# FFN output of six chunks: VectorE 32x32 block turns and SP transfers in place of TensorE transposes

## The chip, the cores and the metric

One core of a Trainium2 chip runs the whole program. The metric is the device time of one execution in microseconds; smaller is better. The kernel before was run three times: 540.84, 541.06 and 541.09 us.

## The reference

The input `x` is 2048 tokens by 128 features, fp32. Three residual steps follow each other, each on the layer-normed `x`:

```python
x = x + 0.5 * ffn(layernorm(x))      # FFN pass 1
x = x + attention(layernorm(x))      # one head, 2048 x 2048 logits
x = x + 0.5 * ffn(layernorm(x))      # FFN pass 2, same weights

# ffn: 64 experts of width 64, top 8 by biased affinity, plus one shared expert
h = silu(einsum('td,edf->etf', xf, W_up))
y = einsum('etf,efd->etd', h, W_down)
out = silu(xf @ Ws_up) @ Ws_down + einsum('etd,te->td', y, cw)
```

`cw` holds the normalised sigmoid gates of a token's eight experts and zero elsewhere. The kernel computes all experts for all tokens and multiplies by `cw`.

## The kernel before

An FFN pass works on four chunks of 512 tokens; chunks are numbered n = 0 to 3 in the first pass and 4 to 7 in the second, and c = n mod 4. In a chunk the tokens lie along the free dimension, the features or hidden rows on the 128 partitions. A chunk is 32 units of two experts each (u = 1 to 32), and a shared-expert unit only where c = 0. Every matrix product is three matmuls of 128x512 (high by low, low by high, high by high parts in the fp32r type).

One unit goes through all engines:

- TensorE: `up(u)`, three matmuls into one of four PSUM buffers, `hid[u mod 4]`; and five units later `down(u)`, three matmuls that accumulate the chunk's y in the PSUM bank `yacc[n mod 2]`. From u = 7 on `up` is issued in pairs, at odd u.
- ScalarE: silu of the hidden buffer (L451), later the high part of the gated product (L462).
- VectorE: `gate_unit`, silu times the gates in `wide` (L718), and the low part (L295) of every third unit (u = 6, 9, 12, 18 and so on). It runs its list strictly in order: the low part of unit u stands right behind the gating of unit u + 1.
- GpSimd: the low part of the other units (L295, and u = 15), out of the buffer `gated`.
- SP: two transfers per unit (L353), each spreading one expert's gates from DRAM over 64 partitions into one of six slots of `wide`. The transfers of unit u wait until unit u - 6 is gated. SP also issues the loads of x and of the weights, the store of the gates (`store_gates`, at u = 30) and the stores of the result. Nothing else is on it, and it also works its list in order.

`up(u + 4)` reuses the buffer of unit u. It waits (`wait_hid_free`) until unit u is gated where GpSimd makes its low part, and until VectorE has made its low part where VectorE does. So `up(16)` waits for the low part of unit 12, which VectorE makes behind the gating of unit 13; `up(22)` waits for the low part of unit 18, made behind the gating of unit 19.

Beside the units, hand-placed by the value of u, run the prologue of the next chunk (layer norm, affinities, top 8, gates: `pro_...`, `joint_...`; on VectorE mostly at u = 13 to 20, absent where c = 3) and the epilogue of the last one. The epilogue of y in chunks n = 1, 2, 3, 5, 6, 7 (it works on y of n - 1) is: ScalarE copies y from PSUM to `yT`, times 0.5, at u = 6 (`epi_y`, L502); TensorE transposes it in four 128x128 matmuls into the bank `mq` at u = 8 (`epi_yT`, through `turn`, L1279); VectorE adds `mq` to x at u = 9 (`epi_x`, L930). In the first pass only (n = 1 to 3), `epi_stats` at u = 10 takes the layer-norm statistics of the new x, four 128x128 pieces (L726, L733), and the keys of the attention follow from u = 20 on. The last chunk of a pass has its own epilogue in halves (`last_...`), in which `yT` is used as before.

The attention between the passes, some 130 us, needs nothing from SP.

Of the kernel before, what the change touches and what calls it, by code (L numbers as in the profile page):

```python
# [31 lines left out]
NB = 6  # L32
EARLY = 6
STORE = 30
GT = 2
# [13 lines left out]
def macaron_kernel(nc, x_d, wup_d, wdn_d, wsup_d, wsdn_d, cent_d, bias_d, wq_d, wk_d, wv_d, gates_d, out_d):  # L49
# [21 lines left out]
    with ExitStack() as ctx:  # L71
# [58 lines left out]
        gated = sb("gated", [P, NG, CH], F32, ffn)  # L130
        yT = sb("yT", [P, CH], F32, ffn)
        xn2 = sb("xn2", [P, TPC, D], F32, ffn)
        gpart = [sb("gpart_hi", [P, NGP, CH], F32R, ffn), sb("gpart_lo", [P, NGP, CH], F32R, ffn)]
# [23 lines left out]
        s_x0b = sem("x_in0_second_half")  # L157
        s_small, s_value, s_qk, s_bias = sem("small_in"), sem("value_in"), sem("qk_in"), sem("bias_in")
        s_eps, s_zero = sem("eps_made"), sem("cw_zeroed")
        j_out, j_aff, j_silu, j_hi, j_lo = (sem("shared_" + n) for n in ("and_aff", "aff_copied", "silu", "hi", "lo"))  # L160
# [152 lines left out]
        def _(sp):  # L313
# [18 lines left out]
            def store_gates(n):  # L332
                sp.wait_ge(s_gates, n + 1)
                sp.dma_start(gates_d[n], gates[:, :]).then_inc(s_gout, 16)

            for n in range(2 * NCH):
                if n % NCH == 0:
                    store_gates(n)
                sp.wait_ge(s_gout, 16 * (n + 1))
                for u in range(1, UNITS):  # L340
                    if early_unit(u, n):
                        continue
                    w = nth_gated(u, n)
                    if n == 0 and u % 2 == 1 and FIRST + (u - NB) // 2 < 2 * WP:
                        load_piece(FIRST + (u - NB) // 2)
                    if n == 0 and u in (24, 28):
                        load_x(u // 4 - 4)
                    if u == STORE and n % NCH != NCH - 1:
                        store_gates(n + 1)
                    if w > NB:  # L350
                        sp.wait_ge(s_gated, w - NB)
                    for e in range(2):
                        sp.dma_start(wide[e * F:(e + 1) * F, slot_of(u, n), :],  # L353
                                     gates_d[n, 2 * u - 2 + e, :].partition_broadcast(F)
                                     ).then_inc(s_wide[slot_of(u, n)], 16)
# [8 lines left out]
        def _(pool):  # L364
# [46 lines left out]
            for f in range(2):  # L411
                for c in range(NCH):
# [6 lines left out]
                    for u in range(min(c, 1), UNITS):  # L419
                        if on_pool(place(u, n)):  # L420
                            low_part(nc.gpsimd, place(u, n)).then_inc(s_glop, 1)
                        if n == 0 and u % 2 == 0 and PRE + u // 2 < 2 * WP:
                            piece_lo(PRE + u // 2)
                        if c + 1 < NCH:
                            if u == 3:
                                rstd(0, n + 1, p_st, p_rs)
                            if u == 18:
                                weights(n + 1)
                            if u == 21:
                                normed_weights(n + 1)  # L430
                        if f == 0 and c and u == 12:
# [7 lines left out]
        def _(act):  # L439
# [57 lines left out]

            def epi_y(n):
                act.wait_ge(s_down, place(PAIRS, n) + 1)
                if n:  # L500
                    act.wait_ge(e_yT, n)
                nc.scalar.mul(yT[:, :], yacc[n % 2][:, :], 0.5).then_inc(e_y, 1)  # L502

            def last_y(n):

                act.wait_ge(s_down, place(UNITS - LAG - 1, n) + 1)
                act.wait_ge(e_yT, n)
                nc.scalar.mul(yT[:, :], yacc[1][:, :], 0.5).then_inc(h_ya, 1)
# [57 lines left out]
            for f in range(2):  # L566
                for c in range(NCH):
# [21 lines left out]
                    for u in range(7 if n == NCH else min(c, 1), UNITS):  # L589
# [19 lines left out]
                        if c:  # L609
                            if u == LAG + 1:  # L610
                                epi_y(n - 1)
                            if f == 0 and u == 27:
                                epi_hi(c - 1)
                            if n == 1 and u == 31:
                                epi_proj_hi(0)
# [79 lines left out]
        def _(dve):  # L695
# [80 lines left out]
            def last_x(h, n, done):  # L776

                dve.wait_ge((h_yT, e_yT)[h], (n // NCH, n)[h] + 1)
                half = x[:, NT - TPC + h * GT:NT - TPC + (h + 1) * GT, :]
# [141 lines left out]
            def pro_sum(n):  # L921
# [4 lines left out]
                nc.vector.reciprocal(inverse_sum(n), wsum[:, 0, :]).then_inc(p_inv, 1)  # L926

            def epi_x(n, c):
                dve.wait_ge(e_yT, n + 1)
                nc.vector.tensor_tensor(x[:, c * TPC:(c + 1) * TPC, :], x[:, c * TPC:(c + 1) * TPC, :],  # L930
                                        mq[:, :].rearrange("p (t d) -> p t d", d=D), ALU.add).then_inc(e_x, 1)

# [39 lines left out]
            for f in range(2):  # L972
                for c in range(NCH):
# [25 lines left out]
                    for u in range(5 if n == NCH else min(c, 1), UNITS):  # L999
# [35 lines left out]
                        if c:  # L1035
                            if u == 9:
                                epi_x(n - 1, c - 1)
                            if f == 0:
                                if u == 10:
                                    epi_stats(c - 1)  # L1040
                                if u == 20:
# [3 lines left out]
                                if u == 21:  # L1045
                                    normed(1, c - 1, c - 1, xn2, e_rs, e_xn, (2, 3))
                                if u == 27:
# [123 lines left out]
        def _(pe):  # L1171
# [78 lines left out]
            def joint_product(n):  # L1250

                pe.wait_ge(p_lo, n + 1)
                if n % NCH > 1:
                    pe.wait_ge(e_x, n - 1)
                else:
# [46 lines left out]
            def pro_cw(n):  # L1302
# [3 lines left out]
                else:  # L1306
                    for i in range(TPC):
                        ins = nc.tensor.transpose(mp[0:E, i * P:(i + 1) * P], cw2[:, i, 0:E], ident[:, :])
                    ins.then_inc(p_cwT, 1)

            def epi_yT(n):
                pe.wait_ge(e_y, n + 1)
                pe.wait_ge(j_lo, joint(n + 1))
                if 0 < n < NCH:
                    pe.wait_ge(e_prlo, 1)
                    pe.wait_ge(e_lo, n)
                elif n == 0:
                    pe.wait_ge(w_Alo, 1)
                else:
                    pe.wait_ge(e_x, n)  # L1320
                turn(yT, mq, e_yT)

# [75 lines left out]
            for f in range(2):  # L1398
                for c in range(NCH):
# [12 lines left out]
                    for u in range(LEADS[1] if n == NCH else min(c, 1), UNITS):  # L1412
# [24 lines left out]
                        if c:  # L1437
                            if u == 8:
                                epi_yT(n - 1)
                            if f == 0:  # L1440
                                if u == 26:
                                    epi_xT(c - 1)
                                if u == 30 and c == 1:
                                    epi_proj(0)
# [157 lines left out]
```

## Time and profile before

| | before |
|---|---|
| times of three runs, us | 540.84, 541.06, 541.09 |
| profiled execution, us | 541.02 |
| its span, first to last instruction, us | 539.2 |
| TensorE busy, share of the span | 99% |
| VectorE, ScalarE, GpSimd busy | 76%, 75%, 51% |
| chain of work that ended last: TensorE's part | 93% |
| transfers of gates into `wide` | 488, of 128 KB |

The span is counted from the first to the last instruction; 1.8 us of the execution lie around it. Busy time of matmuls counts overlapping ends, so it says that TensorE had something under way, not that it ran at its peak. SP doesn't appear among the busy engines: it only issues transfers, and its rows stand in the timeline as SPq, with the time that one issue kept the sequencer.

### The profile page before, as it was taken

The page shows a single profiled execution, that of the slowest core. Times are in us where ns is not written, and L with a number is a line of the kernel's source. Part 1 is how long each engine was busy: PE and PEld are TensorE (multiplying, and loading weights), DVE is VectorE, ACT ScalarE, POOL GpSimd, SP SyncE. Part 2 cuts the span into 40 slices and gives each one's busy share as a digit, 9 for nine tenths or more (in the row PEclk, how much of TensorE's full clock was granted, in tenths as well). Part 3 has the DMA queues.
Part 4 walks back from the last instruction along what each step waited for, and adds up shares of the span by engine and source line. Part 5 has one row for each costly group of instructions (what it writes and reads, how often), then busy time and mean ns, then how long its engine had stood idle before and what let it go on. Part 6 is the DMA issues. An engine that isn't in the chain of part 4 may idle for free.

```text
span 539.2 us, 8716 instructions
## 1 busy us (share of the span) xinstructions
PE 532.0 (99%) x2710; PEld 437.2 (81%) x2710; DVE 408.5 (76%) x933; ACT 407.0 (75%) x815; POOL 273.7 (51%) x242
## 2 busy tenths in 40 slices
PE   8999999999999999999999999999999999999997
PEld 6677887887888888799999999878887888788886
DVE  5998689877966677867777889779678767965664
ACT  6898778877877775866666657778779777877773
POOL 3689757775776764000000000267676676766663
PEclk9999999999999999999999999999999999999999
DMA  8675555554555550000000000155565565556662
GB/s 264 194 220 200 189 182 167 179 197 150 172 187 193 190 160 1 2 1 0 1 2 1 2 1 0 50 193 171 166 195 169 168 202 169 182 157 204 202 193 84
DMA packets 44270, 72.25 MB, mean 134 GB/s; under 512 B 8864, under 2 KB 9632, under 8 KB 44224
## 3 DMA queue, kind: packets, MB, share of 16 engines
q1 hardware_dynamic: 43568, 71.17, 42.0%
q10 hardware_dynamic: 592, 0.39, 0.3%
q8 instruction: 21, 0.34, 0.3%
q0 software_dynamic: 64, 0.13, 0.1%
q14 instruction: 25, 0.20, 0.1%
HBM read 69.57 MB, written 2.10 MB: 133 GB/s over the span
## 4 chain that ended last, share of the span: by engine, by line
PE 93%; DVE 3%; ACT 2%; issue 1%; POOL 0%; DVEq 0%; POOLq 0%
PE lrow L1174 13%; PE lrow L1175 13%; PE lrow L1176 13%; PE bank L1216 11%; PE bank L1218 10%; PE bank L1217 10%; PE bank L1279 5%; PE bank L1501 3%; PE bank L1503 3%; PE bank L1502 3%; PE bank L1393 1%; PE bank L1286 1%; PE bank L1175 1%; PE bank L1176 1%; PE bank L1174 1%
## 5 line engine op out<-in xcount | busy, mean ns | idle before, releaser
L295 POOL TENSOR_TENSOR gpart_lo<-gated,gpart_hi 128x512 fp32r<-128x512 f32 x174 | 223.7, 1295 | 162.9 <-ACT gpart_hi L462 161.3
L451 ACT ACTIVATE lrow<-lrow 128x512 f32<-128x512 f32 (+1 forms) x245 | 143.9, 587 | 62.4 <-PE lrow L1176 61.9
L718 DVE TENSOR_TENSOR gated<-lrow,wide 128x512 f32<-128x512 f32 x170 | 116.1, 683 | 56.3 <-ACT lrow L451 53.6
L462 ACT CAST gpart_hi<-gated 128x512 fp32r<-128x512 f32 x174 | 106.7, 613 | 5.9 <-DVE gated L718 5.3
L1216 PE MATMUL bank<-gpart_lo,wdn_hi 128*128 128x512 f32 x246 | 97.7, 397 | 0.0
L1218 PE MATMUL bank<-gpart_hi,wdn_hi 128*128 128x512 f32 x246 | 97.7, 397 | 0.0
L1217 PE MATMUL bank<-gpart_hi,wdn_lo 128*128 128x512 f32 x246 | 97.0, 394 | 0.0
L718 DVE TENSOR_TENSOR lrow<-lrow,wide 128x512 f32<-128x512 f32 x74 | 51.4, 695 | 26.9 <-ACT lrow L451 26.9
L1092 DVE TENSOR_TENSOR pT_lo<-bank,pT_hi 128x512 fp32r<-128x512 f32 x64 | 43.6, 683 | 21.7 <-ACT pT_hi L650 21.7
L295 DVE TENSOR_TENSOR gpart_lo<-lrow,gpart_hi 128x512 fp32r<-128x512 f32 (+1 forms) x83 | 56.5, 681 | 1.6 <-ACT gpart_hi L462 1.3
L650 ACT CAST pT_hi<-bank 128x512 fp32r<-128x512 f32 x64 | 38.1, 595 | 24.1 <-PE bank L1279 23.9
L1216 PEld LDWEIGHTS bank<-gpart_lo,wdn_hi 128*128 128x128 f32 x246 | 46.2, 188 | 11.3
L1218 PEld LDWEIGHTS bank<-gpart_hi,wdn_hi 128*128 128x128 f32 x246 | 46.2, 188 | 11.1
L1217 PEld LDWEIGHTS bank<-gpart_hi,wdn_lo 128*128 128x128 f32 x246 | 46.1, 188 | 11.0
L643 ACT ACTIVATE prow<-lrow,nmax 128x512 f32<-128x512 f32 x63 | 43.7, 696 | 14.3 <-DVE nmax L964 14.3
L462 ACT CAST gpart_hi<-lrow 128x512 fp32r<-128x512 f32 (+1 forms) x83 | 49.1, 592 | 6.8 <-DVE lrow L718 6.5
L1174 PE MATMUL lrow<-xnT_lo_a,wup_hi 128*128 128x512 f32 x128 | 52.0, 406 | 0.5 <-POOL wdn_lo L382 0.3
L1174 PE MATMUL lrow<-xnT_lo_b,wup_hi 128*128 128x512 f32 x128 | 51.2, 400 | 0.2 <-DVE gpart_lo L295 0.2
L1176 PE MATMUL lrow<-xnT_hi_a,wup_hi 128*128 128x512 f32 x128 | 50.8, 396 | 0.0
L1175 PE MATMUL lrow<-xnT_hi_b,wup_lo 128*128 128x512 f32 x128 | 50.6, 395 | 0.0
L1175 PE MATMUL lrow<-xnT_hi_a,wup_lo 128*128 128x512 f32 x128 | 50.5, 395 | 0.0
L1176 PE MATMUL lrow<-xnT_hi_b,wup_hi 128*128 128x512 f32 x128 | 50.1, 391 | 0.0
(281 smaller groups left out, 978.2 us busy)
## 6 DMA issues: line engine op xcount, KB each, us to landing
wide<-gates_dram SPq DMA_DIRECT2D x488, 128.0 KB, 3.0
raw<-in_w_up SPq DMA_DIRECT2D x8, 256.0 KB, 5.5
raw<-in_w_down SPq DMA_DIRECT2D x8, 256.0 KB, 5.7
gates_dram<-gates SPq DMA_DIRECT2D x8, 128.0 KB, 2.3
x<-in_x SPq DMA_DIRECT2D x3, 256.0 KB, 3.9
out_dram<-x SPq DMA_DIRECT2D x3, 256.0 KB, 3.1
x<-in_x SPq DMA_DIRECT2D x1, 128.0 KB, 2.3
x<-in_x ACTq DMA_DIRECT2D x1, 128.0 KB, 2.5
```

Source lines behind the costliest of these rows:

```text
L295: return eng.tensor_tensor(gpart[1][0:m, U % NGP, :], gated_at(U)[0:m, :], gpart[0][0:m, U % NGP, :].bitcast(F32), ALU.subtract)
L451: nc.scalar.activation(dst[0:m, :], hid[U % NH][0:m, :], ACT.Silu).then_inc(s_silu, 1)
L462: nc.scalar.copy(gpart[0][0:m, U % NGP, :], gated_at(U)[0:m, :]).then_inc(s_ghi, 1)
L643: nc.scalar.activation(prow[:, j * CH:(j + 1) * CH], logit_bank(t, j), ACT.Exp, bias=nmax[:, t % 2:t % 2 + 1], accum_out=psums[:, t, j:j + ...
L718: nc.vector.tensor_tensor(gated_at(U), a, b, ALU.mult).then_inc(s_gated, 1)
L1092: nc.vector.tensor_tensor(pT[1][at], tb[q % 2][:, :].rearrange("p (k n) -> p k n", n=P), pT[0][at].bitcast(F32), ALU.subtract).then_inc(a_ ...
L1174: nc.tensor.matmul(out, a[0], b[1], start=True, stop=False)
L1175: nc.tensor.matmul(out, a[1], b[0], start=False, stop=False)
L1176: return nc.tensor.matmul(out, a[0], b[0], start=False, stop=True)
L1216: nc.tensor.matmul(y, w[0], g[1], start=(U % (NCH * PAIRS + 1) == 0), stop=False)
L1217: nc.tensor.matmul(y, w[1], g[0], start=False, stop=False)
L1218: nc.tensor.matmul(y, w[0], g[0], start=False, stop=(u == (UNITS - 1 if n % NCH < NCH - 1 else UNITS - LAG - 1))).then_inc(s_down, 1)
```

## The change

For y of the six chunks n - 1 with n = 1, 2, 3, 5, 6, 7:

- `epi_y` (ScalarE, u = 6) and `epi_yT` (TensorE, u = 8) are gone. VectorE, at u = 7, turns `yacc` straight from PSUM in 32x32 blocks into a new SBUF tile `y_blocks` (`y_turned`). A block turned in its place puts the tokens on partitions, but only within the block.
- SP, at u = 13, ahead of the two gate transfers of unit 13, waits for that and issues sixteen SBUF to SBUF transfers (`move_y`), each of 32 partitions by 4 pieces of 32 elements (128 bytes), 16 KB in all. They put the blocks where they belong in a new tile `y_tok`, by tokens.
- VectorE, now at u = 16, waits for all sixteen and adds 0.5 times `y_tok` to x (`epi_x`). The statistics move from u = 10 to u = 17, their follow-up on GpSimd from 12 to 18, and the rest of the first pass's epilogue by one unit.
- On TensorE the waits that stood in `epi_yT` stand in part in `joint_product`, which writes the same bank.

```diff
+            def move_y(n):
+
+                sp.wait_ge(e_y, n + 1)
+                to = y_tok[:, :, :].rearrange("p i (b d) -> p i b d", d=SQ)
+                by = y_blocks[:, :].rearrange("p (i k d) -> p i k d", i=TPC, d=SQ)
+                for b in range(P // SQ):
+                    for k in range(P // SQ):
+                        sp.dma_start(to[k * SQ:(k + 1) * SQ, :, b, :], by[b * SQ:(b + 1) * SQ, :, k, :]).then_inc(s_ytok, 16)
...
+                    if u == 13 and n % NCH:
+                        move_y(n - 1)
...
-            def epi_y(n):
-                act.wait_ge(s_down, place(PAIRS, n) + 1)
-                if n:
-                    act.wait_ge(e_yT, n)
-                nc.scalar.mul(yT[:, :], yacc[n % 2][:, :], 0.5).then_inc(e_y, 1)
...
-                            if u == LAG + 1:
-                                epi_y(n - 1)
...
+            def y_turned(n):
+
+                dve.wait_ge(s_down, place(PAIRS, n) + 1)
+                nc.vector.transpose(y_blocks[:, :], yacc[n % 2][:, :]).then_inc(e_y, 1)
+
             def epi_x(n, c):
-                dve.wait_ge(e_yT, n + 1)
-                nc.vector.tensor_tensor(x[:, c * TPC:(c + 1) * TPC, :], x[:, c * TPC:(c + 1) * TPC, :],
-                                        mq[:, :].rearrange("p (t d) -> p t d", d=D), ALU.add).then_inc(e_x, 1)
+
+                dve.wait_ge(s_ytok, 16 * (P // SQ) ** 2 * (n - n // NCH + 1))
+                nc.vector.scalar_tensor_tensor(out=x[:, c * TPC:(c + 1) * TPC, :], in0=y_tok[:, :, :], scalar=0.5,
+                                               in1=x[:, c * TPC:(c + 1) * TPC, :], op0=ALU.mult, op1=ALU.add).then_inc(e_x, 1)
...
-                            if u == 9:
+                            if u == 7:
+                                y_turned(n - 1)
+                            if u == 16:
                                 epi_x(n - 1, c - 1)
                             if f == 0:
-                                if u == 10:
+                                if u == 17:
                                     epi_stats(c - 1)
...
                 if n % NCH > 1:
-                    pe.wait_ge(e_x, n - 1)
+                    pe.wait_ge(j_lo, joint(n - 1))
...
-            def epi_yT(n):
-                pe.wait_ge(e_y, n + 1)
-                pe.wait_ge(j_lo, joint(n + 1))
...
-                turn(yT, mq, e_yT)
...
-                            if u == 8:
-                                epi_yT(n - 1)
```

## Rows read from the trace of the kernel before

**Rows 1.** The page: busy time, and the chain that ended last by engine.
```profile
PE 532.0 (99%) x2710; PEld 437.2 (81%) x2710; DVE 408.5 (76%) x933; ACT 407.0 (75%) x815; POOL 273.7 (51%) x242
...
PE 93%; DVE 3%; ACT 2%; issue 1%; POOL 0%; DVEq 0%; POOLq 0%
```

**Rows 2.** Stretch 84 to 93 us: VectorE's busy us, then granted clock, DMA share, GB/s.
```profile
84.00:93.00 9.00, 8.87 (x26) 1.00 0.53 178
```

**Rows 3.** SP's timeline: start us, us, then line and count of merged issues.
```profile
59.95 6.35 SPq L353 DMA_DIRECT2D wide<-gates_dram  x10
...
101.17 0.46 SPq L334 DMA_DIRECT2D gates_dram<-gates  x1
101.68 27.42 SPq L353 DMA_DIRECT2D wide<-gates_dram  x38
```

**Rows 4.** Chunk 7: busy us (instructions) of PE, PEld, DVE, ACT, POOL; clock, DMA, GB/s.
```profile
487.00:531.00 44.00, 44.00 (x193) 35.52 (x192) 26.87 (x41) 33.60 (x65) 28.38 (x23) 1.00 0.64 196
```

**Rows 5.** SP's own waits over the whole span.
```profile
SPq L353 <- DVE gated L718: 32.7, 62, 1.3
```

**Rows 6.** Tile yT (ns min/median/max, first to last us), and one stop of the chain.
```profile
L1279 PE MATMUL bank<-ident,yT x24: 270/272/300, 74.1 to 497.5; 128*128 128x128 f32 x24
...
74.24 0.48 PE bank L1279 x4
```

**Rows 7.** VectorE's timeline in chunk 2: add and statistics at their old place.
```profile
126.71 0.68 DVE L930 TENSOR_TENSOR x<-x,bank 128x512 f32<-128x512 f32 x1
...
128.50 0.86 DVE L726 BATCH_NORM_STATS2 stat<-x 128x6 f32<-128x128 f32 x4
129.40 0.38 DVE L733 BATCH_NORM_AGGREGATE mv<-stat 128x2 f32<-128x6 f32 x4
```

**Rows 8.** Timeline, chunk 1: low of 6, gating of 13, low of 18, up(22).
```profile
73.08 0.68 DVE L295 TENSOR_TENSOR gpart_lo<-lrow,gpart_hi 128x512 fp32r<-128x512 f32 x1
...
83.00 0.69 DVE L718 TENSOR_TENSOR gated<-lrow,wide 128x512 f32<-128x512 f32 x1 [1.04 <-ACT lrow L451]
...
92.40 0.69 DVE L295 TENSOR_TENSOR gpart_lo<-lrow,gpart_hi 128x512 fp32r<-128x512 f32 x1
...
93.36 0.40 PE L1174 MATMUL lrow<-xnT_lo_a,wup_hi 128*128 128x512 f32 x1
```

**Rows 9.** The same four instructions in chunk 5.
```profile
401.17 0.68 DVE L295 TENSOR_TENSOR gpart_lo<-lrow,gpart_hi 128x512 fp32r<-128x512 f32 x1
...
410.40 0.69 DVE L718 TENSOR_TENSOR gated<-lrow,wide 128x512 f32<-128x512 f32 x1 [1.52 <-ACT lrow L451]
...
419.96 0.68 DVE L295 TENSOR_TENSOR gpart_lo<-lrow,gpart_hi 128x512 fp32r<-128x512 f32 x1
...
421.34 0.39 PE L1174 MATMUL lrow<-xnT_lo_b,wup_hi 128*128 128x512 f32 x1
```

**Rows 10.** The tile raw: weight loads issued by SP, ns min/median/max.
```profile
L326 SPq DMA_DIRECT2D raw<-in_w_up x8: 333/473/628, 2.6 to 23.7; - x8
```

**Rows 11.** The page's DMA issues: median us from issue to landing at the end.
```profile
wide<-gates_dram SPq DMA_DIRECT2D x488, 128.0 KB, 3.0
```

**Rows 12.** Timeline, chunk 3: low of 6, gating of 13, up(16).
```profile
170.43 0.68 DVE L295 TENSOR_TENSOR gpart_lo<-lrow,gpart_hi 128x512 fp32r<-128x512 f32 x1
...
178.55 0.69 DVE L718 TENSOR_TENSOR gated<-lrow,wide 128x512 f32<-128x512 f32 x1 [0.74 <-ACT lrow L451]
...
180.54 0.39 PE L1174 MATMUL lrow<-xnT_lo_a,wup_hi 128*128 128x512 f32 x1
```

**Rows 13.** Timeline, chunk 7: low of 6, gating of 13, low of 12, up(16).
```profile
496.62 0.68 DVE L295 TENSOR_TENSOR gpart_lo<-lrow,gpart_hi 128x512 fp32r<-128x512 f32 x1
...
504.71 0.69 DVE L718 TENSOR_TENSOR gated<-lrow,wide 128x512 f32<-128x512 f32 x1 [1.09 <-ACT lrow L451]
505.32 0.68 DVE L295 TENSOR_TENSOR gpart_lo<-lrow,gpart_hi 128x512 fp32r<-128x512 f32 x1
...
506.68 0.39 PE L1174 MATMUL lrow<-xnT_lo_b,wup_hi 128*128 128x512 f32 x1
```

More of the change, by code:

```diff
@@ L33 @@
 EARLY = 6
+SQ = 32
 STORE = 30
@@ L131, in macaron_kernel @@
         yT = sb("yT", [P, CH], F32, ffn)
+        y_blocks, y_tok = sb("y_blocks", [P, CH], F32, ffn), sb("y_tok", [P, TPC, D], F32, ffn)
         xn2 = sb("xn2", [P, TPC, D], F32, ffn)
@@ L158, in macaron_kernel @@
         s_small, s_value, s_qk, s_bias = sem("small_in"), sem("value_in"), sem("qk_in"), sem("bias_in")
+        s_ytok = sem("y_by_token")
         s_eps, s_zero = sem("eps_made"), sem("cw_zeroed")
@@ L430, in _ @@
                                 normed_weights(n + 1)
-                        if f == 0 and c and u == 12:
+                        if f == 0 and c and u == 18:
                             rstd(1, c - 1, e_st, e_rs)
@@ L496, in pro_cwT @@
                 nc.scalar.copy(gates[:, :], mp[0:E, :]).then_inc(s_gates, 1)
-            def epi_y(n):
-                act.wait_ge(s_down, place(PAIRS, n) + 1)
-                if n:
-                    act.wait_ge(e_yT, n)
-                nc.scalar.mul(yT[:, :], yacc[n % 2][:, :], 0.5).then_inc(e_y, 1)
             def last_y(n):
                 act.wait_ge(s_down, place(UNITS - LAG - 1, n) + 1)
-                act.wait_ge(e_yT, n)
+                if n // NCH:
+                    act.wait_ge(e_yT, n // NCH)
                 nc.scalar.mul(yT[:, :], yacc[1][:, :], 0.5).then_inc(h_ya, 1)
@@ L609, in _ @@
                         if c:
-                            if u == LAG + 1:
-                                epi_y(n - 1)
-                            if f == 0 and u == 27:
+                            if f == 0 and u == 28:
                                 epi_hi(c - 1)
-                            if n == 1 and u == 31:
+                            if n == 1 and u == 32:
                                 epi_proj_hi(0)
@@ L776, in last_x @@
             def last_x(h, n, done):
-                dve.wait_ge((h_yT, e_yT)[h], (n // NCH, n)[h] + 1)
+                dve.wait_ge((h_yT, e_yT)[h], n // NCH + 1)
                 half = x[:, NT - TPC + h * GT:NT - TPC + (h + 1) * GT, :]
@@ L1035, in _ @@
                         if c:
-                            if u == 9:
+                            if u == 7:
+                                y_turned(n - 1)
+                            if u == 16:
                                 epi_x(n - 1, c - 1)
                             if f == 0:
-                                if u == 10:
+                                if u == 17:
                                     epi_stats(c - 1)
-                                if u == 20:
+                                if u == 21:
                                     if c > 1:
@@ L1044, in _ @@
                                     normed(1, c - 1, c - 1, xn2, e_rs, e_xn, (0, 1))
-                                if u == 21:
+                                if u == 22:
                                     normed(1, c - 1, c - 1, xn2, e_rs, e_xn, (2, 3))
-                                if u == 27:
+                                if u == 28:
                                     epi_lo(c - 1)
@@ L1253, in joint_product @@
                 if n % NCH > 1:
-                    pe.wait_ge(e_x, n - 1)
+                    pe.wait_ge(j_lo, joint(n - 1))
+                    if n == 2:
+                        pe.wait_ge(w_Alo, 1)
+                    if n == 3:
+                        pe.wait_ge(e_prlo, 1)
+                        pe.wait_ge(e_lo, 1)
                 else:
@@ L1437, in _ @@
                         if c:
-                            if u == 8:
-                                epi_yT(n - 1)
                             if f == 0:
-                                if u == 26:
+                                if u == 27:
                                     epi_xT(c - 1)
-                                if u == 30 and c == 1:
+                                if u == 31 and c == 1:
                                     epi_proj(0)
```

7 lines of the change are left out of this document (removed).

## The prediction

> **What bounds the kernel now.** I read the page first. TensorE has work under way for 99% of the span and makes 93% of the chain that ended last [rows 1], so a matmul taken out counts in full and idle time elsewhere is free, as long as it stays idle. I then looked for engines that are close behind. From 84 to 93 us, in the prologue part of chunk 1, VectorE is busy for 8.87 of 9.00 us, with TensorE's granted clock at 1.00 (its 2.4 GHz level) and the DMA engines busy for 0.53 of the time [rows 2]. Last comes SP, which the page's busy times leave out. Its timeline shows ten gate transfers issued in 6.35 us, 0.64 each with the pause between them [rows 3]. A unit needs two, 1.28 us, and takes TensorE six matmuls; chunk 7 runs 193 of them in 44 us [rows 4], 0.23 each, 1.37 to 1.40 a unit. So SP is the engine closest to its limit. It waits for VectorE only 32.7 us in 62 waits, half a microsecond each [rows 5].
>
> **What goes.** TensorE's 24 transposes [rows 6] hold the chain for 0.48 us at the first stop, four at a time. With 0.44 to 0.48 that is 6 x 0.46 = 2.8 us. ScalarE's copy isn't on the path: nothing.
>
> **What is added on VectorE at u = 7.** A turn of 128x512 from PSUM. No row shows one. Other 128x512 reads of PSUM take 0.68 us, and the next starts 0.60 after them [rows 7]; I take 0.60 on the queue and 0.68 to its end; twice that is the other end, none the lower. The page of the Trainium skill "Vector Engine (DVE) Microarchitecture Reference" (on the reshape block) says that a turn sustains one element per cycle and lane, which as an estimate gives much the same. It hides: the engine idles 1.0 to 1.5 us before the gating of unit 13 [rows 8, 9].
>
> **What is moved on VectorE.** The add (0.68, so 0.60 on the queue) and in the first pass the statistics (0.86 + 0.38 = 1.24) [rows 7] go from u = 9 and 10 to u = 16 and 17. What they leave is filled with idle time ahead of unit 13 [rows 8], so nothing is won there. Where they arrive VectorE is full [rows 2]: + 1.8 us in front of the low part of unit 18 in chunks 1 and 2, + 0.6 in 5 and 6. That low part ends at 93.09 in chunk 1 and up(22), which waits for it, starts at 93.36 [rows 8]: cover 0.27. In chunk 5 it ends at 420.64 and up(22) starts at 421.34 [rows 9]: cover 0.7. Chunks 3 and 7 have no prologue and hide it.
>
> **What is added on SP at u = 13.** Sixteen issues. Their price decides the case, and no row shows one like them. Three prices are near: a weight load, 128 runs as here but of 2 KB, 0.473 median and so 0.52 with its pause, 0.333 at the least [rows 10]; the store of the gates, the only one of these that reads SBUF, 0.51 from its start to the next; the gate transfer, 0.64 [rows 3]. I take 0.51, the plain copy out of SBUF: 16 x 0.51 = 8.2 us. The ends are 0.38 (0.333 and a pause of 0.05), 6.1 us, and 0.64, 10.2 us. Queued behind them are the two gate transfers of unit 13 and then all later ones, and VectorE waits for those in order: gating of 13, low part of 12, prologue, gating of 14 and so on. A transfer lands 3.0 us after its issue starts [rows 11].
>
> The page "DMA: Bandwidth & Descriptors" of the Trainium skill (Issuing engines are not separate DMA queues) calls the sequencer's time to start a transfer "usually small relative to the DMA itself". Here it is 0.60 of 3.0 us, but the first is paid one after the other and fills nine tenths of the unit; by that rule the sixteen would cost nothing, which is the first rival below.
>
> **Chunk 1, step by step.** VectorE makes the low part of unit 6 at 73.08 [rows 8]; the turn starts at 73.68 and ends at 74.36. SP starts at 74.4 and is through at 82.6, starts the second transfer of unit 13 at 83.2, and it lands at 86.2. Gating of 13 started at 83.00 [rows 8]: 3.2 us late. VectorE ran without a pause from there to the low part of 18 [rows 2], so that ends at 93.09 + 3.2 + 1.8 = 98.1, and up(22) starts 4.7 us later than at 93.36. The 0.46 that TensorE saved at u = 8 is inside that wait and isn't taken off again. Chunk 2 is built alike: 4.7.
>
> **Chunk 5.** Low part of 6 at 401.17, turn done at 402.45, SP through at 410.7, landed at 414.3; the gating of 13 is 3.9 late (it was at 410.40). The low part of 18 ended at 420.64 after an idle 0.2, so it ends at 420.64 + 3.9 + 0.6 - 0.2 = 424.9, and up(22) is 3.6 late [rows 9]. Chunk 6 alike: 3.6.
>
> **Chunk 3.** No prologue, and the units follow each other faster. Low part of 6 at 170.43, turn done at 171.7, SP through at 179.95, landed at 183.6, the gating 5.0 late. Here the first that TensorE misses is the low part of 12, 0.6 behind the gating and 0.68 long: it ends at 184.9, where up(16) started at 180.54 [rows 12]: 4.3 late. **Chunk 7** the same way: 496.62, 497.9, 506.15, 509.8; the low part of 12 ends at 511.1 and up(16) stood at 506.68: 4.4 late [rows 13].
>
> After that the units run at TensorE's 1.40 again and SP, at 1.28, draws level within the chunk: no second wait. Sum: 2 x 4.7 + 4.3 + 2 x 3.6 + 4.4 = 25.3 us. The profiled execution took 541.02 us (span 539.2 and 1.8 around it), the median of the runs is 541.06: 541.1 + 25.3 = 566.4, said as 566. Every 0.1 us in the price of an issue is 1.6 us in each chunk, 9.6 in all: 0.38 gives 554, 0.64 gives 579.
>
> **The rivals.**
>
> *The issues are nearly free, so faster.* A small local copy might leave SP in a tenth of a microsecond or two. The sum then falls with the price until the waits are gone in 3, 5, 6 and 7, which happens below some 0.24 (4.4 / 16 = 0.27 under 0.51); there each gives back its 0.46. The moved statistics would still hold up(22) in chunks 1 and 2 by 1.8 - 0.27 = 1.5 each: 541.1 + 3.0 - 1.8 = 542.3. Only if they find cover too is it 541.1 - 2.8 = 538.3. For it: the transfers are small and go from SBUF to SBUF. Against it: no issue on SP took under 0.33 [rows 10], whatever its size. Chance 0.05 for 538, 0.03 for about 542.
>
> *An issue is paid by its runs.* The gate transfer has 64 runs in 0.64 us, 0.01 each; a move has 128 on each side, 1.28 us. Sixteen take 20.5 us, 12.3 more in each chunk: 566 + 74 = 640, with SP the bound of six chunks. Against it: the weight load has 128 runs and takes half a microsecond [rows 10]. A mild form, 0.75, gives 589. The same page of the skill (Specifications) says that pieces under 512 B are read, changed and written back. If that held the DMA engines up, 2048 pieces over 16 engines would have to take more than 8.2 / 128 = 64 ns each to outlast the issues, and then the gate transfers would land late by the difference. Chance for this group 0.14, half of it within 592.
>
> *TensorE's clock falls.* The waits in chunks 3 and 7 are over 4 us in one piece, and the trace has nothing like it after the start. If the granted clock fell to 1.2 GHz after each of six waits and stayed there for some 5 us, half of that is lost, 2.5 each: 566 + 15 = 581. Nothing in the trace shows a fall [rows 2], but nothing tests it. Chance 0.10.
>
> *The same price, 0.33 to 0.40.* 549 to 556. Chance 0.10.
>
> *The forecast itself,* 0.45 to 0.65 an issue: 560 to 580, chance 0.58.
>
> **How the numbers follow.** The range of 552 to 592 leaves out the free issues, the lower half of the cheap ones and the dear half of the second rival, some 0.2 in all. Of six chunks none can come out far below the rows' bounds unless the issue does. About 0.2% is what measurement can tell from no change. Faster 0.05, within 0.2% 0.03, slower 0.92.
>
> **What would show it.** SP's timeline must show sixteen issues in a row at the start of unit 13, 7 to 10 us long, and the first gate transfer only behind them. VectorE must wait for a DMA into `wide` ahead of the gating of 13 in six chunks; the page before has no such wait. TensorE must wait for VectorE's low part before up(16) in chunks 3 and 7, and by up(22) in 1, 2, 5 and 6, some 4 us a chunk. `y_tok` must have landed before VectorE asks for it. If SP issues a move in under 0.25 us the forecast is wrong from its first step; if VectorE waits for `y_tok` instead, the pieces of 128 bytes are what is dear; if the granted clock shows below 1.00, the third rival adds.

## The result and the profile after

The changed kernel takes 589.73 us (median of four runs, 587.59 to 591.18) where the kernel before took 540.95: 1.090 times as long, with an interval of 1.087 to 1.093. That is 48.8 us more. The forecast had 25 more, in a range that ends at 592; its own band for the mechanism it expected, 560 to 580, was missed.

The page of the kernel after, its busy times, the granted clock in forty slices and the chain by engine (compare [rows 1]):

```profile
PE 543.3 (92%) x2686; PEld 442.4 (75%) x2686; DVE 414.5 (71%) x939; ACT 405.5 (69%) x809; POOL 274.2 (47%) x242
...
PEclk9999997999899789999999999999997998999799
...
PE 72%; SPq 11%; DVE 8%; ACT 3%; DMA 3%; issue 2%; POOL 0%; DVEq 0%; POOLq 0%
```

TensorE ran 24 matmuls fewer and has 11 us more of busy time, because part of them ran at the lower clock. A tenth of the chain that ended last is now SP's queue, which had no part in it before.

The list of waits (engine, line, releaser: us in total, times, longest us) has three rows that the kernel before doesn't have at this size:

```profile
DVE gated L725 <- DMA wide<-gates_dram: 54.8, 9, 9.7
...
PEld lrow L1189 <- DVE gpart_lo L298: 42.8, 13, 7.3
PE lrow L1189 <- DVE gpart_lo L298: 37.6, 8, 6.8
```

VectorE waits for gates, 9.7 us at the longest, and TensorE waits for VectorE's low part (its weight loads and its matmuls wait together, so the two rows are one stall). The cause is in SP's timeline of chunk 1, and its effect in VectorE's and TensorE's:

```profile
69.41 3.79 SPq L367 DMA_DIRECT2D wide<-gates_dram  x6
74.58 11.38 SPq L346 DMA_DIRECT2D y_tok<-y_blocks  x16
86.01 18.02 SPq L367 DMA_DIRECT2D wide<-gates_dram  x27
```

```profile
73.85 0.71 DVE L938 STREAM_TRANSPOSE y_blocks<-bank 128x512 f32<-128x512 f32 x1
...
79.70 0.70 DVE L725 TENSOR_TENSOR lrow<-lrow,wide 128x512 f32<-128x512 f32 x1 [0.32 <-ACT lrow L465]
90.06 0.69 DVE L725 TENSOR_TENSOR gated<-lrow,wide 128x512 f32<-128x512 f32 x1 [9.66 <-DMA wide<-gates_dram]
90.67 0.68 DVE L298 TENSOR_TENSOR gpart_lo<-lrow,gpart_hi 128x512 fp32r<-128x512 f32 x1
```

```profile
84.52 0.40 PE L1191 MATMUL lrow<-xnT_hi_a,wup_hi 128*128 128x512 f32 x1
91.40 0.79 PE L1189 MATMUL lrow<-xnT_lo_a,wup_hi 128*128 128x512 f32 x1 [6.48 <-DVE gpart_lo L298]
91.99 0.63 PE L1190 MATMUL lrow<-xnT_hi_a,wup_lo 128*128 128x512 f32 x1
92.42 0.63 PE L1191 MATMUL lrow<-xnT_hi_a,wup_hi 128*128 128x512 f32 x1
```

The turn ends at 74.56 and SP starts at 74.58. Sixteen issues hold it to 85.96, and only then does it issue the gates of unit 13. Their second half lands at 90.06, VectorE gates unit 13, makes the low part of unit 12 behind it, and up(16) starts as that ends. TensorE stood idle for 6.48 us, and its matmuls come back at 0.43 us from start to start where 0.23 was usual: the lower level of 1.2 GHz.

The DMA engines themselves had little to do meanwhile. Two stretches of the same kernel, during the sixteen issues and before them (length, busy us of PE, PEld, DVE, ACT, POOL, granted clock, DMA share, GB/s):

```profile
76.00:85.00 9.00, 8.91 (x40) 6.62 (x38) 3.77 (x6) 6.79 (x13) 3.85 (x3) 1.00 0.18 25
60.00:74.00 14.00, 14.00 (x64) 11.25 (x64) 11.19 (x31) 11.12 (x23) 9.72 (x9) 1.00 0.61 203
```

The tile `y_tok` (issue time min/median/max in ns, then landing) shows that no one waited for y itself; a move lands 1.8 us after its issue starts:

```profile
L346 SPq DMA_DIRECT2D y_tok<-y_blocks x96: 600/601/1776, 74.6 to 547.7; - x96
L943 DVE SCALAR_TENSOR_TENSOR x<-y_tok,x x6: 730/742/1340, 96.3 to 556.9; 128x512 f32<-128x512 f32 x6
...
DMA to landing us min/median/max: 1.8/1.8/3.2
```

The six chunks, from the timelines. "Growth" is how much longer the stretch from the gating of this chunk's unit 7 to that of the next chunk's is than before (chunk 7: to the gating of its unit 32).

| chunk | SP's sixteen, us | gating of 13 late | growth | forecast, 0.51 an issue | same sum, issues as measured |
|---|---|---|---|---|---|
| 1 | 11.4 | 6.9 | 8.9 | 4.7 | 7.9 |
| 2 | 10.3 | 5.4 | 7.1 | 4.7 | 6.8 |
| 3 | 10.3 | 7.2 | 9.2 | 4.3 | 6.4 |
| 5 | 10.3 | 6.3 | 7.1 | 3.6 | 5.7 |
| 6 | 11.5 | 7.6 | 7.7 | 3.6 | 6.9 |
| 7 | 10.3 | 7.3 | 8.4 | 4.4 | 6.5 |
| sum | | | 48.4 | 25.3 | 40.2 |

Chunk 4, which has no moves, is unchanged (46.33 us against 46.41). So the loss is all in the six chunks, and 40 of 48 us of it come out of the forecast's sum once the issues are put in as measured.

### The profile page after: what moved, and what is told of

It is laid out like the page before. It is cut to its first block, busy times and chain, and to the rows that moved or that the text cites. A ratio compares the mean times of both kernels' runs of the same rounds, so it can differ in the third digit from the quotient of the medians.

```text
span 587.7 us, 8751 instructions
## 1 busy us (share of the span) xinstructions
PE 543.3 (92%) x2686; PEld 442.4 (75%) x2686; DVE 414.5 (71%) x939; ACT 405.5 (69%) x809; POOL 274.2 (47%) x242
## 4 chain that ended last, share of the span: by engine, by line
PE 72%; SPq 11%; DVE 8%; ACT 3%; DMA 3%; issue 2%; POOL 0%; DVEq 0%; POOLq 0%
PE lrow L1189 10%; SPq L346 10%; PE lrow L1190 10%; PE lrow L1191 10%; PE bank L1231 8%; PE bank L1232 7%; PE bank L1233 7%; PE bank L1299 5%; DMA wide<-gates_dram 3%; PE bank L1507 3%; PE bank L1509 3%; PE bank L1508 3%; DVE gated L725 2%; DVE gpart_lo L298 2%; ACT lrow L465 1%
## 5 line engine op out<-in xcount | busy, mean ns | idle before, releaser
L1231 PE MATMUL bank<-gpart_lo,wdn_hi 128*128 128x512 f32 x246 | 100.7, 409 | 0.0
L1233 PE MATMUL bank<-gpart_hi,wdn_hi 128*128 128x512 f32 x246 | 99.6, 405 | 0.0
L1232 PE MATMUL bank<-gpart_hi,wdn_lo 128*128 128x512 f32 x246 | 99.5, 405 | 0.0
L1189 PE MATMUL lrow<-xnT_lo_a,wup_hi 128*128 128x512 f32 x128 | 53.9, 421 | 19.5 <-DVE gpart_lo L298 18.8
L1189 PE MATMUL lrow<-xnT_lo_b,wup_hi 128*128 128x512 f32 x128 | 52.6, 411 | 18.8 <-DVE gpart_lo L298 18.8
L1231 PEld LDWEIGHTS bank<-gpart_lo,wdn_hi 128*128 128x128 f32 x246 | 47.9, 195 | 11.9
L1233 PEld LDWEIGHTS bank<-gpart_hi,wdn_hi 128*128 128x128 f32 x246 | 47.6, 194 | 11.7
L1232 PEld LDWEIGHTS bank<-gpart_hi,wdn_lo 128*128 128x128 f32 x246 | 47.9, 195 | 11.2
L1190 PE MATMUL lrow<-xnT_hi_a,wup_lo 128*128 128x512 f32 x128 | 51.8, 405 | 0.0
```

The lines of the kernel that those rows point to most:

```text
L1189: nc.tensor.matmul(out, a[0], b[1], start=True, stop=False)
L1190: nc.tensor.matmul(out, a[1], b[0], start=False, stop=False)
L1231: nc.tensor.matmul(y, w[0], g[1], start=(U % (NCH * PAIRS + 1) == 0), stop=False)
L1232: nc.tensor.matmul(y, w[1], g[0], start=False, stop=False)
L1233: nc.tensor.matmul(y, w[0], g[0], start=False, stop=(u == (UNITS - 1 if n % NCH < NCH - 1 else UNITS - LAG - 1))).then_inc(s_down, 1)
```

## The experiments

The theory: SP's queue is held by sixteen issues, the gates behind them come late, and VectorE and TensorE wait in order. Rivals: the moved and added work on VectorE carries a good part; the cost is that of pieces of 128 bytes, in the issue or on the DMA engines; the fall of TensorE's clock carries a good part.

**Without the moves.**

```diff
-                    if u == 13 and n % NCH:
-                        move_y(n - 1)
...
-                dve.wait_ge(s_ytok, 16 * (P // SQ) ** 2 * (n - n // NCH + 1))
+                dve.wait_ge(e_y, n + 1)
...
```

> The changed kernel without the sixteen transfers; the add on VectorE reads y_blocks where it lies (so y is left out of its place by tokens). All else as changed: the turn at u = 7, the add at 16, the statistics at 17, no transposes on TensorE. If the issues on SP are the cause, nearly all is gone: 542.3 by the forecast's sum for a price of zero (six times 0.46 given back, twice 1.5 lost before up(22) of chunks 1 and 2), granted clock 1.00. If the turn or the moved work on VectorE carried a good part, it stays over 550.

Measured: 542.01 us (ratio 1.0013, interval 0.9997 to 1.0028), clock 0.999. The forecast's sum for a price of zero gave 542.3. The wait that it put at up(22) is there; TensorE's and VectorE's timelines of chunk 1 in this run:

```profile
94.88 0.50 PE L1187 MATMUL lrow<-xnT_lo_a,wup_hi 128*128 128x512 f32 x1 [1.15 <-DVE gpart_lo L298]
```

```profile
91.62 0.86 DVE L731 BATCH_NORM_STATS2 stat<-x 128x6 f32<-128x128 f32 x4
92.52 0.38 DVE L738 BATCH_NORM_AGGREGATE mv<-stat 128x2 f32<-128x6 f32 x4
92.81 0.67 DVE L723 TENSOR_TENSOR lrow<-lrow,wide 128x512 f32<-128x512 f32 x1
93.39 0.68 DVE L723 TENSOR_TENSOR gated<-lrow,wide 128x512 f32<-128x512 f32 x1
94.14 0.69 DVE L298 TENSOR_TENSOR gpart_lo<-lrow,gpart_hi 128x512 fp32r<-128x512 f32 x1
```

The low part of unit 18 ends at 94.83 and up(22) starts at 94.88. All that the change does on VectorE, ScalarE and TensorE together comes out at about one microsecond or less. The other 48 are the moves. That the sum met the time within 0.3 us is in part luck. From unit 7 of one chunk to unit 7 of the next, chunks 1 and 2 grew by 0.9 us each where the sum had 1.5, and chunks 3, 5, 6 and 7 shrank by 0.2 to 0.35 where it had 0.46: both terms came out at some 60% of their size, and they have opposite signs.

**The moves alone, on the kernel before.**

```diff
+            def move_y(n):
+                sp.wait_ge(s_whi, 2 * WP)
+                sp.wait_ge(s_gated, (n + 1) * PAIRS + 7)
+                to = y_tok[:, :, :].rearrange("p i (b d) -> p i b d", d=SQ)
+                by = wup[0][:, 0:CH].bitcast(F32).rearrange("p (i k d) -> p i k d", i=TPC, d=SQ)
...
+                    if u == 13 and n % NCH:
+                        move_y(n - 1)
...
```

> The kernel before with its epilogue untouched, and sixteen transfers of the same shape at u = 13 of the same six chunks, out of a weight tile into a tile that nobody reads; SP waits for the gating of unit 7 first. If SP's time alone makes the loss: 571 to 585, because they start some 1.2 us earlier than in the changed kernel (no turn to wait for) and nothing else is late, with VectorE waiting for wide ahead of unit 13 six times. If the loss needs the moved work on VectorE too, under 560.

Measured: 584.54 us (1.079, 1.075 to 1.084). VectorE waited 43.4 us for `wide`. SP's and VectorE's timelines of chunk 1:

```profile
73.26 11.15 SPq L347 DMA_DIRECT2D y_tok<-wup_hi  x16
```

```profile
81.26 0.69 DVE L733 TENSOR_TENSOR lrow<-lrow,wide 128x512 f32<-128x512 f32 x1
88.22 0.69 DVE L733 TENSOR_TENSOR gated<-lrow,wide 128x512 f32<-128x512 f32 x1 [6.27 <-DMA wide<-gates_dram]
```

Transfers that nobody reads cost 43 us of the 49. They start 1.3 us sooner than in the kernel after, as they don't wait for the turn, and the six gatings of unit 13 are 34 us late in sum where they are 41 late there. Together with the run before this one, the moves are needed for the loss and enough for nearly all of it.

**Eight moves in place of sixteen.**

```diff
-                    for k in range(P // SQ):
+                    for k in range(P // SQ // 2):
...
```

> The changed kernel with eight of the sixteen transfers (half of y_tok isn't filled, and the add reads y_blocks in place, so y isn't put by tokens). Queue theory: SP is held 5.2 us in place of 10.3, most of which the load's lead of 5.7 us covers: 541 + 25.3 - 6 x 3.0 = 548, and no fall of the clock. A cost in proportion to the number of transfers or pieces, such as contention: half of 48.8, 565.

Measured: 554.95 us over two runs that differ (552.6 and 557.3; ratio 1.0245, 1.018 to 1.031), clock 1.00 in the profiled one and 0.994 in the other. Half of the moves cost 14 us where all cost 49: there is a lead that covers the first ones, as the queue theory says, but the time lies between its 548 and the 565 of proportion, so this run by itself doesn't decide between them. In the profiled run the six chunks grew by 11.8 us where the sum had 7.3. SP was held 5.25 us in chunk 1, as expected, and the gates landed 3.0 to 3.4 us after their issue. Two us of the difference are one long issue each among the gate transfers behind the moves, 1.54 us in chunk 1 and 1.72 in chunk 6.

**Longer runs, and the whole width.** Two kernels that keep sixteen transfers of 16 KB but change their shape: 32 runs of 512 bytes, and 128 partitions with one run of 128 bytes each.

```diff
-                        sp.dma_start(to[k * SQ:(k + 1) * SQ, :, b, :], by[b * SQ:(b + 1) * SQ, :, k, :]).then_inc(s_ytok, 16)
+                        sp.dma_start(y_tok[k * SQ:(k + 1) * SQ, b, :], y_blocks[b * SQ:(b + 1) * SQ, k * P:(k + 1) * P]).then_inc(s_ytok, 16)
```

> The changed kernel with sixteen transfers of the same 16 KB each in 32 runs of 512 bytes in place of 128 of 128 bytes (blocks land in the wrong place). If the price is per issue, the pitch stays near 0.64 us and the time at 586 to 592. If it is per run, or if the DMA engines' work on pieces of 128 bytes is what is late, the pitch falls to a quarter or the wait for wide shrinks: under 570.

```diff
+                for j in range(CH // SQ):
+                    sp.dma_start(y_tok[:, j // 4, j % 4 * SQ:(j % 4 + 1) * SQ],
+                                 y_blocks[:, j * SQ:(j + 1) * SQ]).then_inc(s_ytok, 16)
```

> The changed kernel with sixteen transfers of the same 16 KB each over all 128 partitions, one run of 128 bytes in each, straight across (nothing is put in its place). If the 0.64 us of a move comes with its shape (32 partitions, four runs in each), the pitch is nearer to the 0.52 of the weight load, 128 partitions wide, SP is held 8.3 us and the time is 569 to 575. If any transfer issued right behind another costs 0.64, it is 585 to 590.

Measured: 586.61 us (1.083, 1.079 to 1.087) and 587.29 us (1.085, 1.082 to 1.089). SP's timeline in chunk 2, long runs first, then the kernel after; and the issue times (ns, min/median/max) of the whole-width moves:

```profile
130.38 10.04 SPq L346 DMA_DIRECT2D y_tok<-y_blocks  x16
```

```profile
132.51 10.32 SPq L346 DMA_DIRECT2D y_tok<-y_blocks  x16
```

```profile
L345 SPq DMA_DIRECT2D y_tok<-y_blocks x96: 488/601/1135, 74.2 to 545.7; - x96
```

A quarter of the runs saves 0.3 us of 10.3. The price is the issue's in all three shapes: 0.59 to 0.60 us and a pause of 0.04. That closes the rival of a price by runs, and with the DMA share of 0.18 above also the one that the DMA engines are late with short pieces. It also shows where the forecast's 0.51 was wrong: a move right behind another cost the 0.64 of a gate transfer in every shape tried, not the 0.51 of the store of the gates. That store always came after a pause of SP of 1.1 us or more, and the trace of the kernel before shows what a pause does to one and the same transfer: 0.44 us for a gate transfer after a pause, 0.60 for the next one right behind it (two views of SP's timeline in chunk 1).

```profile
76.81 0.44 SPq L353 DMA_DIRECT2D wide<-gates_dram  x1
```

```profile
77.30 0.60 SPq L353 DMA_DIRECT2D wide<-gates_dram  x1
```

Over the whole span the gate transfers after a pause of more than 0.5 us have a median of 0.445 us (32 of them), those right behind another issue 0.596 (430). Why some of the weight loads at the start of the program were issued in 0.43 us right behind each other stays open.

**The moves spread out,** two ahead of each of the units 13 to 20, on the kernel with the moves alone.

```diff
-                    if u == 13 and n % NCH:
-                        move_y(n - 1)
+                    if 13 <= u <= 20 and n % NCH:
+                        move_y(n - 1, u - 13)
...
```

> As moves_alone, but two of the sixteen transfers ahead of each of the units 13 to 20. Queue theory: the same 10.3 us of SP, but they reach unit 20 only with SP some 9.4 us late against a lead of 3.8 us of the gates and some 3 us that TensorE can wait: 2.5 us a chunk, 555 to 560, clock 1.00. If what counts is SP's total time (51.8 us a chunk against 47 to 49), 541 + 6 x 4 = 565. If a transfer costs the same wherever it stands, 585 as before.

Measured: 579.82 us (1.071, 1.068 to 1.074), a clear miss. It helped by 5 us, not by 25. VectorE's timeline of chunk 7 up to the low part of unit 18:

```profile
546.41 0.69 DVE L733 TENSOR_TENSOR gated<-lrow,wide 128x512 f32<-128x512 f32 x1 [1.88 <-DMA wide<-gates_dram]
549.08 0.70 DVE L733 TENSOR_TENSOR lrow<-lrow,wide 128x512 f32<-128x512 f32 x1 [1.98 <-DMA wide<-gates_dram]
551.72 0.69 DVE L733 TENSOR_TENSOR gated<-lrow,wide 128x512 f32<-128x512 f32 x1 [1.94 <-DMA wide<-gates_dram]
552.33 0.68 DVE L298 TENSOR_TENSOR gpart_lo<-lrow,gpart_hi 128x512 fp32r<-128x512 f32 x1
```

Each unit now takes 2.7 us, two moves and two gate transfers of SP. Counted from the gating of unit 7, the second transfer of unit 19 is issued 11.4 us later than in the kernel before: 9.4 are the fourteen moves ahead of it at 0.67, 1.1 SP was behind from the start of the chunk, and a long issue is the most of the rest. Before, this transfer was issued 7.0 us ahead of its use, of which the landing takes 3.1, so it had a lead of 4.0. The gating of unit 19 is 7.5 late, and up(22), with a cover of 0.7 as in [rows 9], 6.9. The lead of 3.8 us that I had expected was right. The 3 us that I had granted TensorE as patience weren't there. In this chunk SP's backlog at the low part of unit 18 counts, whether it built up at once or in pieces.

This run also holds a test of the pause that wasn't meant as one: in three of the eight places the store of the gates now comes right behind another issue, and it takes 0.59 to 0.60 us there, and 0.47 to 0.53 in the other five. One of the three:

```profile
162.41 0.60 SPq L337 DMA_DIRECT2D gates_dram<-gates  x1
```

**The clock held up.** Between up(15) and up(16) TensorE runs spare matmuls into the y bank that is free then.

```diff
                             up(u, n)
+                            if u == 15 and c:
+                                pe.wait_ge(e_y, n)
+                                keep_warm(KEEP, yacc[(n + 1) % 2])
                             up(u + 1, n)
```

With KEEP = 24:

> The changed kernel, and between up(15) and up(16) of the six chunks TensorE runs 24 spare matmuls of 256 columns (some 5.2 us by the 0.215 us of the kernel before) into the other y bank, which nobody needs then, in place of most of its wait for the low part of unit 12. If the half clock after the wait costs what lies between unit 16 and unit 32 of a chunk beyond the run without the transfers (1.0 to 2.7 us in each, 9.8 in all), the clock stays at 1.00 and the time falls to 578 to 582. If the fall of the clock is hidden behind SP's late transfers, it stays at 588 to 591.

With KEEP = 12:

> As kept_warm with 12 spare matmuls in place of 24: each of them is two instructions of 0.215 us, so 12 take 5.2 us and end before the low part of unit 12 comes, where 24 took 10.3 and ran past it. The chip's clock should stay at 1.00 and the stretch from up(16) to unit 32 shrink by 1.3 to 2.5 us a chunk, as it did with 24, with up(16) no later than in the changed kernel: 578 to 581. If the half clock costs nothing because VectorE and SP are behind anyway, 589.

Measured: 602.5 us (1.114, 1.111 to 1.116) with 24, and 588.6 us (586.8 to 589.9; 1.087, 1.084 to 1.089) with 12. The first is a slip of mine: each spare matmul is two instructions, and TensorE's timeline of chunk 1 shows them run past the wait that they were to fill:

```profile
84.62 10.52 PE L1356 MATMUL bank<-ident 128*128 128x256 f32 x48
94.79 0.58 PE L1190 MATMUL lrow<-xnT_lo_a,wup_hi 128*128 128x512 f32 x1
```

With 12 the filling ends 1.8 us before the low part comes. Chunk 3 shows what the clock does (kernel after, then kept warm; columns as in the stretches above):

```profile
201.00:229.00 28.00, 25.82 (x102) 20.74 (x103) 19.61 (x41) 18.31 (x35) 18.91 (x17) 0.86 0.56 179
```

```profile
203.00:231.00 28.00, 26.07 (x114) 20.47 (x113) 20.89 (x44) 20.26 (x38) 19.91 (x17) 1.00 0.59 179
```

At a clock of 1.00 TensorE gets through 114 instructions in the same 28 us, three of them spare ones, and through 102 at 0.86. From up(16) to the gating of unit 32 chunk 3 takes 25.35 us in place of 27.53. But the clock wasn't held in all chunks: it fell all the same around up(22) of chunk 2 and behind up(16) of chunk 7. Chunks 6 and 7 of this run:

```profile
498.00:512.00 14.00, 12.03 (x52) 9.12 (x51) 13.25 (x35) 10.19 (x19) 9.84 (x8) 1.00 0.70 204
```

```profile
553.00:567.00 14.00, 13.14 (x50) 10.52 (x51) 9.48 (x14) 9.33 (x18) 8.94 (x7) 0.88 0.63 199
```

That gives a comparison chunk by chunk. How much longer the stretch from the gating of unit 13 to that of unit 32 is than in the run without the moves, in us, from the timelines:

| kernel | the clock fell in chunks | 1 | 2 | 3 | 5 | 6 | 7 |
|---|---|---|---|---|---|---|---|
| after | all six | 0.1 | -0.2 | 2.0 | 0.7 | 0.0 | 1.1 |
| kept warm, 12 | 2 and 7 | -0.3 | 1.3 | -0.1 | -0.3 | -0.2 | 1.0 |
| eight moves | none | -0.3 | -0.2 | -0.5 | -0.3 | -0.2 | -0.5 |

Where the clock held, nothing is lost behind the gating of unit 13. The fall costs the kernel after 5.7 us in sum against the last row, and 3.7 against the four chunks of the middle row that kept their clock: 4 to 6 us, with 41 of the 588 us at half speed by the record of the granted clock. That the time as a whole fell by only 1.1 us, less than the runs of either kernel differ, has a reason that this one profile shows: one of the sixteen issues took 1.57, 1.69 and 1.91 us in chunks 1, 2 and 5, where the kernel after had such issues in chunks 1 and 6, and the gatings of unit 13 came 2.9 us later in sum. The expectation of 578 to 581 was wrong. I had put all of the growth behind up(16), 9.8 us, to the clock, and 6.2 of that is slack of TensorE: without the moves up(16) starts 2.0 to 2.6 us behind the gating of unit 13, in the kernel after 1.3.

**Five issues in place of sixteen.** y_blocks is stored to DRAM in one transfer and loaded by tokens in four.

```diff
+            def store_y(n):
+                sp.wait_ge(e_y, n + 1)
+                sp.dma_start(y_d[n], y_blocks[:, :]).then_inc(s_yst, 16)
+
+            def load_y(n):
+                sp.wait_ge(s_yst, 16 * (n - n // NCH + 1))
+                by = y_d[n].rearrange("(b t) (i k f) -> k t i b f", b=P // SQ, i=TPC, f=SQ)
+                for k in range(P // SQ):
+                    to = y_tok[k * SQ:(k + 1) * SQ, :, :].rearrange("p i (b f) -> p i b f", f=SQ)
+                    sp.dma_start(to, by[k]).then_inc(s_ytok, 16)
...
+LOAD = {1: 14, 2: 14, 3: 14, 5: 16, 6: 16, 7: 24}
+ADD = {1: 12, 2: 12, 3: 13, 5: 22, 6: 22, 7: 28}
...
```

> The changed kernel with five issues in place of sixteen: y_blocks goes to DRAM in one transfer at SP's unit 12, and four transfers by tokens bring it back (at unit 14 in the first pass, 16 and 24 in the second). The turn is at u = 6, the add and the statistics at u = 12 and 13 in the first pass, where VectorE had idle time, the add at 22 and 28 in the second. If an issue costs 0.64 whatever its pieces are, SP is held 3.2 us a chunk, the load's lead covers that, nothing is late and TensorE's 2.8 us come out: 538.2, 537.8 to 539.5. If 512 pieces in one transfer make its issue long or its landing late, over 545.

Measured: 540.07 us (0.9975, 0.9965 to 0.9984), a little less of a gain than expected. In chunk 1 the add waited for `y_tok`, with VectorE behind it:

```profile
82.37 0.69 DVE L951 SCALAR_TENSOR_TENSOR x<-y_tok,x 128x512 f32<-128x512 f32 x1 [2.32 <-DMA y_tok<-y_dram]
```

So the same with the turn at u = 5 and the store and the loads of the first pass one unit earlier:

> As via_dram with the turn at u = 5, the store at SP's unit 11 and, in the first pass, the loads at 13. In via_dram the add of chunk 1 waited 2.3 us for y_tok, and that chunk took 1.25 us more than before in place of 0.46 less. If that wait goes, 1.7 us come back: 538.4, 537.8 to 539.3. If y isn't complete at VectorE's u = 5 or SP stalls on the landing of its store, 540 to 541.

Measured: 538.43 us (six runs, 538.33 to 539.13), 0.9945 of the kernel before (0.9928 to 0.9961). It leaves nothing out and is faster than both kernels. SP's timeline in chunk 1, and the add:

```profile
71.68 0.34 SPq L344 DMA_DIRECT2D y_dram<-y_blocks  x1
72.07 2.37 SPq L375 DMA_DIRECT2D wide<-gates_dram  x4
74.48 2.70 SPq L352 DMA_DIRECT2D y_tok<-y_dram  x4
```

```profile
79.95 0.79 DVE L951 SCALAR_TENSOR_TENSOR x<-y_tok,x 128x512 f32<-128x512 f32 x1
80.77 0.87 DVE L741 BATCH_NORM_STATS2 stat<-x 128x6 f32<-128x128 f32 x4
```

Each of the four loads has 512 pieces of 128 bytes and costs SP 0.67 us with its pause, little more than the 0.64 of a move with 128. The idea of the change was sound; its sixteen issues were not.

## Why the prediction was right or wrong

Faster or slower was called rightly, and so was the path of the loss: SP's queue, the gates, VectorE, TensorE. The size was half of what was measured. The time lies within the range only because that reached up to 592 for a rival, a price by runs, that the long runs then ruled out; that much was luck.

**What bounds the kernel:** right. SP, which no busy time shows, was the engine nearest to its limit, and it set the loss. One reading was too low: by the same view as [rows 5] SP waits for VectorE 52.3 us in 93 waits, as a second row, for units that are gated in place, has 19.6 us in 31.

**The transposes, 2.8 us:** too high. In the run without the moves up(16) of chunk 7 comes 0.31 us sooner after the gating of unit 7, in place of 0.46, and chunks 5 and 6 show the same. The last kernel gains 2.9 in all, but it also has the add and the statistics elsewhere and gains up to 0.8 in one chunk, so that this figure doesn't price the transposes.

**The turn, 0.60 on the queue and 0.68 to its end:** it measured 0.704 and the next instruction started 0.63 behind it. Right, and hidden.

**The moved work, 1.5 us at up(22) of chunks 1 and 2:** right in kind, 0.9 us each as measured without the moves. "Nothing is won" at their old place was wrong: there the gating of unit 13 comes 1.0 us sooner in these two chunks. In the kernel after this doesn't show, since the gates come later than either.

**The price of an issue, 0.51 us:** the step that failed. It measured 0.644, the upper end, and in chunks 1 and 6 one of the sixteen took 1.57 and 1.78. At the sum's own slope this is 15 of the 23.5 us that were missing (the table: 25.3 becomes 40.2). I had chosen the store of the gates because it reads SBUF; the row of ten gate transfers in 6.35 us [rows 3] was the one that showed issues back to back in this stretch. The store's 0.46 was that of an issue after SP had been idle, and I read it as that of its kind: right behind another issue the same store took 0.60 in the run with the moves spread out.

**The landing, 3.0 us:** 3.0 to 3.4 for the gates behind the moves. With it and the turn, the gatings of unit 13 are 40.7 us late in sum, where the forecast's steps with the measured issues give 39.2: 1.4 of the 8.2 us that are still missing.

**"After that no second wait", and the covers:** right where the clock holds. With eight moves and a clock of 1.00 the stretch behind the gating of unit 13 is 0.2 to 0.5 us shorter than without any moves, which is cover of the kind that the forecast took off. In the kernel after no cover shows: up(16) of chunk 7 came 6.7 us late against 6.5 by the sum with measured issues, but the chunk as a whole grew by 8.4. The clock's 4 to 6 us are the most of what is left of the 8.2; the rest, some 1 to 3 us, wasn't taken apart.

**The third rival, the clock:** its mechanism is real and its price was too high. The granted clock fell to 1.2 GHz at the waits of all six chunks, as the rival's sum had it. By the Trainium skill's page "TensorE: Matmul & The Clock Gate" (Part 1) an idle array goes back to that level, and the trace agrees: it idles 6.48 us in chunk 1 and comes back with matmuls 0.43 us apart, and in chunk 3 the clock is 0.83 over the stretch from 190 to 220 us. The forecast priced it at 15 us, 2.5 a chunk; it took between nothing and 2.5, and 4 to 6 in sum. That is far from the 20 us that 41 us at half speed would be worth if TensorE alone set the pace.

**The first two rivals:** free issues are out (no move took under 0.60 us), and a price by runs is out. The sentence of the Trainium skill that starting a transfer is usually short against the transfer ("DMA: Bandwidth & Descriptors", Issuing engines are not separate DMA queues) doesn't hold for these: 0.60 us of issue stand against 1.8 from issue to landing, and sixteen of them add up while the landings overlap.

## What to carry to other kernels

Count the issues of every queue that only issues, as one counts instructions of an engine: here two transfers a unit at 0.64 us each took 1.28 of 1.40 us, and the profile's busy times show nothing of it. Price a new issue by rows of back-to-back issues in the same stretch, not by one that follows a pause, and look for what its successors' consumers do in order behind them. Many small transfers are to be folded into a few with longer patterns, even by way of DRAM: a quarter of the pieces saved 0.3 of 10.3 us on the queue here, and five issues in place of sixteen, with the turn and the add placed anew, took away the whole loss.

## What the runs showed of the hardware that was not expected

- The time that an issue keeps SP is nearly the same, 0.59 to 0.64 us right behind another issue, for 32 runs of 512 bytes, 128 of 128 bytes in two shapes, and 512 of 128 bytes out of DRAM. After a pause the shapes differ: 0.63 us for the moves of the kernel after, 0.54 for the long runs, 0.49 for the whole width, 0.44 for a gate transfer, and 0.33 for the store of y to DRAM, which took 0.52 to 0.59 right behind another.
- Now and then one issue takes 1.0 to 1.9 us. It isn't the moves: the kernel before has ten of 1.0 to 1.6 us, all gate transfers, mostly 23 to 32 us apart. In every kernel with sixteen moves at u = 13 one fell into the moves of chunk 1 (1.57, 1.34, 1.04, 1.14, 1.61 and 1.57 us). Its cause is open.
- VectorE's add of two SBUF tiles, 128x512 fp32, took 0.73 to 0.74 us in four chunks of the kernel after and 1.34 and 1.27 in chunks 3 and 7, while the add that reads PSUM took 0.68 in all six chunks of the kernel before. The two long ones run beside a low part on GpSimd for 0.7 to 0.8 us, the four short ones for 0.2. In the other kernels too no such add over 0.8 us was without one beside it for 0.7 us or more, but some with as much beside them took 0.69 to 0.80. Whether GpSimd's work is the reason wasn't tested.
